# A four-layer graph network on one core: a new layout for the third layer's split values, and run masks computed in the passes before it

## The chip, the core and the metric

The kernel runs on one NeuronCore of a Trainium2 chip. The core has TensorE (PE in the profile; its weight loads are PEld), VectorE (DVE), ScalarE (ACT), GpSimd (POOL), SyncE (SP) and 16 DMA engines. They run side by side and meet only at semaphores. The metric is the device time of one execution in microseconds (us), lower is better.

## The reference

There are 6250 nodes with 64 features, and 200,000 edges sorted by their target. Four layers follow each other; each adds its result to x and normalises the rows.

```python
x = _layernorm(x + _L0_gnn_ref(x, edge_index, ...))   # mean over neighbours, two dense layers
x = _layernorm(x + _L1_gnn_ref(x, edge_index))        # neighbours weighted by 1/sqrt(deg*deg)
x = _layernorm(x + _L2_gnn_ref(x, edge_index, ...))   # the third layer
x = _layernorm(x + _L3_gnn_ref(x, edge_index, ...))   # the fourth: attention
# third layer (_L2), after Wh = h @ W + b, row, col = src, dst
dot = jnp.sum(Wr * Wc, axis=-1)
sim = dot / jnp.maximum(nr * nc, EPS)
prop_pos = jax.ops.segment_sum((base * sim_pos)[:, None] * Wc, row, num_segments=n_nodes)
prop_neg = jax.ops.segment_sum((base * sim_neg)[:, None] * Wc, row, num_segments=n_nodes)
# fourth layer (_L3)
m = jax.ops.segment_max(alpha, dst, num_segments=n)
a = jnp.exp(alpha - m[dst])
a = a / (s[dst] + 1e-16)
out = jax.ops.segment_sum(a[:, None] * x_j, dst, num_segments=n) + bias
```

## The kernel before

The nodes make 49 blocks of 128. The edges are sorted into 49 x 49 pairs of (target block, source block) with up to 128 edges each; `G` is 7, so a block is worked in 7 groups of 7 pairs, and layers three and four have 343 such steps each. Gathers and scatters are matmuls with one-hot matrices. To keep f32 accuracy, a f32 number is split into three bf16 words (its upper half, the upper half of the remainder, and the rest), each multiplied by itself and summed in PSUM.

The stages in order of time: the head with the first layer (`pairs_*`, up to about 1240 us), which also stores a count matrix `AD`, the edges' rows `ROWS` and `ROWS3`, and the one-hot matrices `OND` and `OSD` in HBM; two passes over `AD` (`passes_*`, to about 1736 us: the first sums over the neighbours for the first layer's second half, the second for the second layer), where SP loads one 1568 KB row of `AD` per step into a ring of three and PE runs 49 matmuls on it (L1047); the third layer (`pairs3_*`, to about 2680 us); the fourth (`pairs4_*`, to the end). POOL has no work in the passes.

Every engine has its own instruction list, in the order written; a wait holds all that stands behind it on that engine.

**Third layer.** At step n PE gathers the rows of both ends (`ends`, L1289 and L1296), ACT copies one end out (L1339), DVE multiplies and sums them (L1389, L1394), and DVE makes a coefficient for each edge once per block (L1402 to L1412). Group m then goes: coefficient x value, three of its seven pairs by ACT (`values`, L1348, at step m + 8) and four by POOL (`values`, L1260); POOL takes the remainder over the upper half (`rests`, L1268) and the third word (L1270), two groups in one instruction; PE multiplies with the one-hot of the sources (`spread`, L1308, at step m + 12). POOL's order is values(u), rests(u-1), values(u+1), with u a pair of groups. The three words lie as three planes of f32 in a ring of `NV3` = 6 groups in the tile `EDG`; PE reads the upper halves of each plane, so every second bf16. `values` waits until `spread` has used the group six before. One-hot matrices of the sources wait in `NOS` = 13 buffers; SP loads them (L1237). Every third one-hot matrix of the ends is made by ACT (L1329, L1331), the others by DVE (L1381).

**Fourth layer.** At step t PE gathers group t (L1668) and ACT copies it out (L1606) into a ring of 18; ACT scales seven pairs (L1627, step k + 16), DVE takes the remainder (L1817, k + 17), POOL the third word (L1655, k + 18), PE multiplies with the one-hot of the targets (L1688, k + 19). The scaled values have a ring of `NV` = 4: L1627 waits for the L1688 of four groups before. Once per block comes the chain of the softmax: the maximum over each run of equal targets is a scan (L1841) over a 49 x 128 tile, which needs two masks, one that adds -1e30 where a run begins and one that keeps the last of each run. These are made from the targets: PE turns them (L1695), ACT copies (L1613), POOL works four instructions (L1646, L1648, L1650, L1651). PE turns the scan's result and the second mask back (L1708, L1709); tiny matmuls follow (L1719, L1678) with DVE's reductions between (L1849 to L1872, L1807 to L1813), and ACT's exponential (L1617). DVE also makes one-hot matrices for two groups at a time (L1750 for the gather, L1755 for the targets).

## Time and profile before

| | us |
|---|---|
| median of 3 runs | 3594.78 (3585.97 to 3599.09) |
| the profiled execution | 3591.77 |
| its span, first to last instruction | 3590.0 |

Busy shares of the span: PE 81%, PEld 73%, DVE 81%, ACT 62%, POOL 44%. The page cuts the span in 40 slices of 90 us; the row for POOL is near zero before slice 20, the row of TensorE's clock shows 9 or 8 tenths with a few 7s. "Idle before" in a row is the time in which the engine did nothing just before that instruction, and the engine named is the one whose event ended it. The shares are means over stages with different limits, so the views by stretch are of more use than the page.

### The profile page before, as it was taken

How to read it: one execution, taken by the hardware profiler on the slowest of the kernel's cores; microseconds unless marked ns; L12 is line 12 of the kernel's file. 1: busy time of each engine (PE TensorE's matmuls, PEld its weight loads, DVE VectorE, ACT ScalarE, POOL GpSimd, SP SyncE). 2: the span in 40 equal slices, each digit the busy share in tenths (PEclk: the TensorE clock that was granted, in tenths of full speed). 3: DMA queues.
4: the chain of work that ended last, by engine and by line, in shares of the span. 5: the costliest groups of instructions: out<-in, count | busy, mean ns of one | idle time of the engine just before them, and what ended most of it. 6: DMA issues, size and time to landing. Idle time of an engine off the chain costs nothing.

```text
span 3590.0 us, 122167 instructions
## 1 busy us (share of the span) xinstructions
PE 2911.7 (81%) x50473; PEld 2637.4 (73%) x50473; DVE 2904.2 (81%) x4610; ACT 2219.8 (62%) x6003; POOL 1584.4 (44%) x1253
## 2 busy tenths in 40 slices
PE   0199999999999699899688888787768888888886
PEld 0178888888888599899677777777757777777775
DVE  7599999999999522233688888898857999999997
ACT  6334444444444400001698888898857898899887
POOL 2012222222221000000399988898964655666564
PEclk9999999999999899999899999999977888888887
DMA  8157777777777799898687877787738888888884
GB/s 221 66 157 244 237 232 234 243 237 231 234 243 236 253 370 360 330 328 320 215 279 259 264 264 248 254 271 250 257 124 302 279 278 277 276 290 274 267 278 129
DMA packets 606666, 907.43 MB, mean 253 GB/s; under 512 B 358505, under 2 KB 494858, under 8 KB 587163
## 3 DMA queue, kind: packets, MB, share of 16 engines
q1 hardware_dynamic: 583992, 800.62, 68.1%
q10 hardware_dynamic: 19763, 94.38, 7.1%
q8 instruction: 406, 6.65, 0.7%
q0 software_dynamic: 2352, 4.52, 0.3%
q14 instruction: 153, 1.25, 0.1%
HBM read 651.96 MB, written 247.40 MB: 251 GB/s over the span
## 4 chain that ended last, share of the span: by engine, by line
PE 36%; DVE 27%; ACT 14%; issue 10%; POOL 6%; DMA 5%; ACTq 1%; SPq 0%; DVEq 0%; POOLq 0%
PE ps L683 9%; PE ps L1047 8%; PE ps L709 4%; DMA U<-AD 4%; ACT U L1627 3%; POOL EDG L1268 3%; DVE EDG L1755 3%; DVE U L1817 3%; PE ps L696 3%; ACT U L569 3%; POOL EDG L1260 2%; ACT U L1329 2%; PE ps L667 2%; PE ps L1289 1%; DVE A L1389 1%
## 5 line engine op out<-in xcount | busy, mean ns | idle before, releaser
L569 ACT ACTIVATE U<-ps 128x512 bf16<-128x512 f32 (+1 forms) x637 | 356.4, 573 | 499.5 <-PE ps L696 475.5
L1627 ACT ACTIVATE U<-U,T 128x65 f32<-128x65 f32 x1806 | 460.1, 343 | 47.7 <-PE ps L1688 42.3
L1260 POOL TENSOR_TENSOR EDG<-U,edge 128x512 f32<-128x512 f32 (+1 forms) x196 | 214.3, 1098 | 584.1 <-DVE edge L1412 551.1
L1047 PE MATMUL ps<-U 128*128 128x192 bf16 x4802 | 418.5, 248 | 33.2 <-DMA U<-AD 32.8
L1047 PEld LDWEIGHTS ps<-U 128*128 128x128 bf16 x4802 | 402.8, 98 | 42.5 <-DMA U<-AD 39.2
L1655 POOL TENSOR_TENSOR U<-U 128x455 f32<-128x455 f32 x258 | 296.4, 1152 | 215.3 <-DVE U L1817 215.3
L866 DVE TENSOR_TENSOR EDG<-edge,EDG 128x1792 bf16<-128x1792 bf16 x343 | 367.5, 1083 | 14.4 <-DMA OSD<-EDG 12.0
L502 POOL DMA_INDIRECT U<-REC,nod x49 | 94.0, 1918 | 622.4 <-PE ps L638 501.2
L683 PE MATMUL ps<-U 128*128 128x98 bf16 (+1 forms) x5292 | 363.5, 223 | 4.5 <-DVE U L854 3.5
L709 PE MATMUL ps<-EDG,U 128*128 128x193 bf16 x2401 | 311.4, 249 | 51.1 <-ACT U L569 39.9
L683 PEld LDWEIGHTS ps<-U 128*128 128x128 bf16 x5292 | 341.3, 98 | 15.7 <-DVE U L854 11.9
L1296 PE MATMUL ps<-U 128*128 128x65 bf16 x7203 | 287.2, 195 | 72.3 <-DVE A L1389 71.8
L1270 POOL TENSOR_TENSOR EDG<-EDG 128x896 f32<-128x896 f32 (+1 forms) x172 | 312.4, 1817 | 13.5
L1268 POOL TENSOR_TENSOR EDG<-EDG 128x896 f32<-128x896 f32 (+1 forms) x172 | 308.6, 1794 | 11.7 <-ACT EDG L1348 11.7
L1296 PEld LDWEIGHTS ps<-U 128*128 128x128 bf16 x7203 | 252.1, 98 | 80.5 <-DVE A L1389 80.1
L1289 PE MATMUL ps<-U 128*128 128x65 bf16 x7203 | 289.6, 195 | 13.8 <-ACT U L1331 8.0
L1389 DVE TENSOR_TENSOR A<-ps,U 128x455 f32<-128x455 f32 x343 | 210.4, 622 | 95.7 <-ACT U L1339 77.0
L1289 PEld LDWEIGHTS ps<-U 128*128 128x128 bf16 x7203 | 271.3, 98 | 18.5 <-issue 10.1
L1348 ACT ACTIVATE EDG<-U,edge 128x64 f32<-128x64 f32 x1029 | 279.3, 338 | 9.0 <-PE ps L1308 6.1
L1139 DVE TENSOR_REDUCE A<-ps 128x64 f32<-128x192 f32 x98 | 34.3, 355 | 294.3 <-PE ps L1047 294.0
L854 DVE TENSOR_TENSOR U<-U 128x3920 bf16<-128x3920 bf16 (+1 forms) x132 | 263.7, 2000 | 0.0
L1381 DVE TENSOR_SCALAR U<-U,iotap 128x1792 bf16<-128x1792 bf16 x228 | 252.7, 1109 | 1.5 <-DMA U<-ROWS 1.5
(323 smaller groups left out, 7019.4 us busy)
## 6 DMA issues: line engine op xcount, KB each, us to landing
U<-ROWS SPq DMA_DIRECT2D x411, 448.0 KB, 4.7
U<-AD SPq DMA_DIRECT2D x98, 1568.0 KB, 8.6
OND<-EDG SPq DMA_DIRECT2D x343, 224.0 KB, 2.8
OSD<-EDG SPq DMA_DIRECT2D x343, 224.0 KB, 3.6
AD<-U ACTq DMA_DIRECT2D x49, 1568.0 KB, 5.6
EDG<-ROWS SPq DMA_DIRECT2D x171, 448.0 KB, 6.3
U<-OND SPq DMA_DIRECT2D x303, 224.0 KB, 5.9
U<-OSD SPq DMA_DIRECT2D x213, 224.0 KB, 4.7
```

The costliest lines, as they stand in the source:

```text
L569: ev4.by(act.activation(prow[i % NPW][:, P * g:P * (g + m)], ps[4 + gg % 2][:, 0:P * m], ACT.Copy))
L683: ins = pe.matmul(ps[3][:, o:o + NB * (f1 - f0)], w_, FR[h][:, c, f0:f1, :, k], start=(h + c + k + f0 == 0), stop=(last and f0 == 0))
L709: ins = pe.matmul(ps[6][:, 0:XW], prow[i % NPW][:, P * j:P * j + P], Xs[:, j, :], start=(j == 0), stop=(j == NB - 1))
L866: hot8.by(dve.tensor_tensor(HOT[r].rearrange("p s c (r k) -> p (s c) r k", k=2), bc(r1v.unsqueeze(1), [P, 14, D, 2]), bc(sdb[i % 2][:, b, ...
L1047: ins = pe.matmul(ps[q][:, 0:192], arow[r][:, P * j:P * j + P], (XsB if p else XsA)[:, j, :, :].rearrange("p s f -> p (s f)"), start=(j == ...
L1260: ins = pool.tensor_tensor(VD[:, v:v + w, 0, KA * D:G * D].rearrange("p w (k f) -> p w k f", f=D), W_, bc(c_.unsqueeze(3), [P, w, G - KA, ...
L1268: rem3.by(pool.tensor_tensor(VD[:, v:v + w, 1, :], VD[:, v:v + w, 0, :], VH[:, v:v + w, 0, :], ALU.subtract))
L1270: low3.by(pool.tensor_tensor(VD[:, v:v + w, 2, :], VD[:, v:v + w, 1, :], VH[:, v:v + w, 1, :], ALU.subtract))
L1289: ins = pe.matmul(ps[h][:, 65 * k:65 * k + 65], rw[r][:, 2 * P * k + P:2 * P * k + 2 * P], Ws[:, i0 + k, s_, 0:65], start=(s_ == 0), stop= ...
L1296: ins = pe.matmul(ps[2 + h][:, 65 * k:65 * k + 65], rw[r][:, 2 * P * k:2 * P * k + P], Ws[:, j, s_, 0:65], start=(s_ == 0), stop=(s_ == 2))
L1627: ins = act.activation(V4[k % NV][:, 0, c, :], H[k % NHR][:, c, :], ACT.Copy, scale=a4[d % 2][:, s:s + 1])
L1655: look.by(pool.tensor_tensor(V4[k % NV][:, 2, :, :], V4[k % NV][:, 1, :, :], S4[k % NV][:, 1, :, :], ALU.subtract))
```

## The change

Third layer. The ring holds 8 groups of 2 words per element (value and remainder side by side, 8 bytes) where it held 6 groups of 3 planes. The third word is written as bf16 into the lower half of the remainder's word, which nobody reads. So ACT and POOL write the value with a step of 8 bytes, POOL reads and writes the remainder with the same step, POOL writes 2-byte third words with a step of 8 bytes, and PE reads three adjacent bf16 of each four. The space that falls free takes two more one-hot buffers (`NOS` = 15). DVE's sum of the three words reads PSUM with the words adjacent.

Run masks. A new `passes_pool` computes both masks for all 49 blocks from `ROWS3` during the passes, seven blocks at a time, and SP stores them as bf16 in HBM (`MSK`), between its loads of `AD` in the second pass. The fourth layer loads 49 x 256 bf16 per block instead. The transposition L1695, the copy L1613 and POOL's four instructions leave it; the turning of the second mask becomes one bf16 matmul. The helpers `value_at` and `rest_at` come with empty tables, which leaves their waits as before.

```diff
+        MSK = dram("MSK", (NB, NB, 2, P), BF16)
...
+        mdst = EDG[0:NB, 0:3136].bitcast(BF16)[:, 0:NB * P].rearrange("p (d r) -> p d r", r=P)
+        mboth = EDG[0:NB, 3136:9408].bitcast(BF16).rearrange("p (d m r) -> p d m r", m=2, r=P)
+        mdif = U[0:NB, upper + NB * 96:upper + NB * 96 + GB * 129].rearrange("p (d r) -> p d r", r=129)
+        def passes_pool(pool):
+            msk_d.by(pool.memset(mdif[:, :, 0:1], 1.0))
+            msk_d.by(pool.memset(mdif[:, :, P:P + 1], 1.0))
+            pool.wait_ge(msk_ld.at, msk_ld.o + 16)
+            for g in range(NGB):
...
+                msk_d.by(pool.tensor_tensor(mdif[:, :, 1:P], mdst[:, bl, 1:P], mdst[:, bl, 0:P - 1], ALU.subtract))
+                pool.wait_ge(msk_d.at, msk_d.o + 4 * g + 3)
+                msk_d.by(pool.tensor_scalar(mdif, mdif, 0.0, 1.0, ALU.is_equal, ALU.subtract))
+                pool.wait_ge(msk_d.at, msk_d.o + 4 * g + 4)
+                msk_ok.by(pool.tensor_scalar(mboth[:, bl, 0, :], mdif[:, :, 0:P], BIG, None, ALU.mult))
+                msk_ok.by(pool.tensor_scalar(mboth[:, bl, 1, :], mdif[:, :, 1:P + 1], -1.0, None, ALU.mult))
+            pool.wait_ge(msk_st.at, msk_st.o + 16 * NGB)
         def passes_sp(sp):
+            msk_ld.by(sp.dma_start(mdst, ROWS3[1].rearrange("d (s r) -> s d r", r=P)), 16)
             for p in range(2):
                 for i in range(NB):
+                    if p and i % GB == GB - 1:
+                        g = i // GB
+                        sp.wait_ge(msk_ok.at, msk_ok.o + 2 * g + 2)
+                        msk_st.by(sp.dma_start(MSK[GB * g:GB * g + GB].rearrange("d s m r -> s d (m r)"),
+                                               mboth[:, GB * g:GB * g + GB, :, :].rearrange("p d m r -> p d (m r)")), 16)
...
-        NV3 = 6
-        VD = EDG[:, 0:3 * G * D * NV3].rearrange("p (v s e) -> p v s e", v=NV3, s=3)
-        VH = EDG[:, 0:3 * G * D * NV3].bitcast(BF16).rearrange("p (v s e h) -> p v s e h", v=NV3, s=3, h=2)[:, :, :, :, 1]
+        NV3 = 8
+        VD = EDG[:, 0:2 * G * D * NV3].rearrange("p (v e w) -> p v e w", v=NV3, w=2)
+        VH = EDG[:, 0:2 * G * D * NV3].bitcast(BF16).rearrange("p (v e h) -> p v e h", v=NV3, h=4)
...
-                rem3.by(pool.tensor_tensor(VD[:, v:v + w, 1, :], VD[:, v:v + w, 0, :], VH[:, v:v + w, 0, :], ALU.subtract))
+                rem3.by(pool.tensor_tensor(VD[:, v:v + w, :, 1], VD[:, v:v + w, :, 0], VH[:, v:v + w, :, 1], ALU.subtract))
                 pool.wait_ge(rem3.at, rem3.o + u + 1)
-                low3.by(pool.tensor_tensor(VD[:, v:v + w, 2, :], VD[:, v:v + w, 1, :], VH[:, v:v + w, 1, :], ALU.subtract))
+                low3.by(pool.tensor_tensor(VH[:, v:v + w, :, 2], VD[:, v:v + w, :, 1], VH[:, v:v + w, :, 3], ALU.subtract))
...
-                    ins = pe.matmul(ps[4 + j % 2][:, 0:3 * D], OSn[m % NOS][:, k, :], S3[m % NV3][:, :, k, :], start=(i == 0), stop=(i == NB - 1))
+                    ins = pe.matmul(ps[4 + j % 2][:, 0:3 * D], OSn[m % NOS][:, k, :], VH[:, m % NV3, D * k:D * k + D, 1:4], start=(i == 0), stop=(i == NB - 1))
...
-                    ins = act.activation(V3[m % NV3][:, 0, k, :], Wc[:, j % 2, i0 + k, 0:D], ACT.Copy, scale=edge[:, 6 + j % 2, i0 + k:i0 + k + 1])
+                    ins = act.activation(VD[:, m % NV3, D * k:D * k + D, 0], Wc[:, j % 2, i0 + k, 0:D], ACT.Copy, scale=edge[:, 6 + j % 2, i0 + k:i0 + k + 1])
...
+            def run_masks(d):
+                if d >= 2:
+                    sp.wait_ge(ytr.at, ytr.o + d - 1)
+                mk_ld[d % 2].by(sp.dma_start(masks[d % 2], MSK[d]), 16)
...
-                    ytr.by(pe.transpose(ps[3][:, 64:64 + NB], lastf, ident[0:NB, 0:NB]))
+                    ytr.by(pe.matmul(ps[3][:, 64:64 + NB], masks[d % 2][:, 1, :], identh, start=True, stop=True))
...
-                    dvf.by(dve.tensor_tensor_scan(ysc, negs, ps[2][0:NB, 0:P], -BIG, ALU.add, ALU.max))
+                    dve.wait_ge(mk_ld[d % 2].at, mk_ld[d % 2].o + 16 * (d // 2 + 1))
+                    dvf.by(dve.tensor_tensor_scan(ysc, masks[d % 2][:, 0, :], ps[2][0:NB, 0:P], -BIG, ALU.add, ALU.max))
```

## Rows read from the trace of the kernel before

**Rows 1.** Busy time by stretch: passes, third layer, a steady 100 us, fourth layer.

```profile
core 0: us, PE busy (x) PEld busy (x) DVE busy (x) ACT busy (x) POOL busy (x), PEclk, DMA share, GB/s
1240.00:1480.00 240.00, 212.92 (x2469) 206.62 (x2470) 75.02 (x162) 16.70 (x35) 0.00 (x0) 0.96 0.91 350
1480.00:1736.00 256.00, 230.27 (x2483) 216.74 (x2480) 88.36 (x225) 26.19 (x79) 0.00 (x0) 0.96 0.82 300
1753.00:2665.00 912.00, 722.79 (x16548) 688.60 (x16549) 762.18 (x1111) 795.74 (x1678) 824.22 (x540) 0.97 0.77 254
1790.00:1890.00 100.00, 80.80 (x1972) 78.57 (x1973) 85.78 (x124) 92.21 (x191) 95.98 (x64) 1.00 0.83 279
...
2740.00:3540.00 800.00, 660.30 (x13553) 607.26 (x13554) 753.28 (x1706) 717.12 (x2661) 482.94 (x502) 0.88 0.84 277
```

**Rows 2.** Groups by line, 1753 to 2665 us, POOL, then one of ACT.

```profile
L1270 POOL TENSOR_TENSOR EDG<-EDG 128x896 f32<-128x896 f32 (+1 forms) x172 | 312.4, 1817 | 13.5
L1268 POOL TENSOR_TENSOR EDG<-EDG 128x896 f32<-128x896 f32 (+1 forms) x172 | 308.6, 1794 | 11.7 <-ACT EDG L1348 11.7
L1260 POOL TENSOR_TENSOR EDG<-U,edge 128x512 f32<-128x512 f32 (+1 forms) x196 | 214.3, 1098 | 584.1 <-DVE edge L1412 551.1 <-PE ps L1308 32.7
...
L1348 ACT ACTIVATE EDG<-U,edge 128x64 f32<-128x64 f32 x1029 | 279.3, 338 | 9.0 <-PE ps L1308 6.1 <-DVE edge L1412 2.9
```

**Rows 3.** Waits in the same stretch, POOL: total, times, longest, in us.

```profile
POOL EDG L1260 <- PE ps L1308: 32.7, 23, 5.3
```

**Rows 4.** Groups by line and shape in the first 150 us: ACT, then DVE.

```profile
L255 ACT ACTIVATE U<-U 128x1568 bf16<-128x1568 int32 x1 | 7.2, 7175 | 0.0
...
L251 ACT ACTIVATE EDG<-EDG 128x1568 f32<-128x1568 f32 x1 | 1.5, 1510 | 0.0
...
L401 DVE TENSOR_TENSOR U<-EDG,U 128x1568 f32<-128x1568 f32 x1 | 3.0, 2980 | 8.2 <-ACT U L261 8.2
...
L386 DVE TENSOR_TENSOR EDG<-EDG,A 128x1568 f32<-128x1568 f32 x1 | 1.8, 1791 | 0.0
```

**Rows 5.** Groups by line, 2740 to 3540 us (46 blocks): POOL, then DVE.

```profile
L1655 POOL TENSOR_TENSOR U<-U 128x455 f32<-128x455 f32 x238 | 275.7, 1161 | 191.7 <-DVE U L1817 191.7
...
L1648 POOL TENSOR_SCALAR MISC<-T 49x129 f32<-49x129 f32 x46 | 39.5, 860 | 4.0
L1646 POOL TENSOR_TENSOR T<-MISC 49x127 f32<-49x127 f32 x46 | 33.7, 732 | 10.0 <-ACT MISC L1613 9.6
L1651 POOL TENSOR_SCALAR T<-MISC 49x128 f32<-49x128 f32 x46 | 30.5, 663 | 3.6
L1650 POOL TENSOR_SCALAR T<-MISC 49x128 f32<-49x128 f32 x46 | 24.4, 530 | 3.8
...
L1755 DVE TENSOR_SCALAR EDG<-EDG,iotap 128x1792 bf16<-128x1792 bf16 x160 | 149.8, 936 | 5.4 <-DMA EDG<-ROWS 5.4
```

**Rows 6.** Timeline of one block's mask work and what follows, DVE, then POOL.

```profile
3152.91 2.77 DVE L1755 TENSOR_SCALAR EDG<-EDG,iotap 128x1792 bf16<-128x1792 bf16 x1
...
3152.44 0.94 POOL L1651 TENSOR_SCALAR T<-MISC 49x128 f32<-49x128 f32 x1
3153.35 0.94 POOL L1655 TENSOR_TENSOR MISC<-MISC 128x455 f32<-128x455 f32 x1
3154.25 0.94 POOL L1655 TENSOR_TENSOR U<-U 128x455 f32<-128x455 f32 x1
```

**Rows 7.** Timeline: the passes' first loads and matmuls, and two small stores of ROWS.

```profile
1241.20 3.12 SPq L999 DMA_DIRECT2D U<-AD  x3
...
1248.75 1.46 PE L1047 MATMUL ps<-U 128*128 128x192 bf16 x8 [14.78 <-DMA U<-AD]
...
1226.59 0.27 ACTq L558 DMA_DIRECT2D ROWS<-EDG  x1
1226.89 1.25 ACTq L559 DMA_DIRECT2D ROWS<-EDG  x1
```

**Rows 8.** The line L1755: count, duration in ns as minimum/median/maximum.

```profile
L1755 DVE TENSOR_SCALAR EDG<-EDG,iotap x172: 442/681/2770, 2702.9 to 3553.2; 128x1792 bf16<-128x1792 bf16 x171, 128x896 bf16<-128x896 bf16 x1
```

More of the change, by code:

```diff
@@ L1496, in cell @@
             return rows[k // 2 % n][:, e:e + P]
-        seg, negs, lastf, ylast = (Tflat[0:NB, 1225 + 130 * n:1225 + 130 * n + w] for n, w in enumerate((129, P, P, P)))
+        ylast = Tflat[0:NB, 1615:1615 + P]
+        masks = [MISC[0:NB, 1365 + P * i:1365 + P * i + P].bitcast(BF16).rearrange("p (m r) -> p m r", m=2) for i in range(2)]
+        identh = ident[0:NB, 0:NB].bitcast(BF16).rearrange("p (r h) -> p r h", h=2)[:, :, 1]
         ysc = ps[3][0:NB, P:2 * P]
@@ L1533, in due4, with value_at, rest_at @@
             return (k // G, k % G, k) if 0 <= k < NT else (None, None, None)
+        GV, GR = (), ()
+        def value_at(eng, k):
+            d, g = k // G, k % G
+            if g in GV:
+                eng.wait_ge(vop.at, vop.o + d * len(GV) + GV.index(g) + 1)
+            else:
+                eng.wait_ge(vok.at, vok.o + d * (G - len(GV)) + sum(h not in GV for h in range(g + 1)))
+        def rest_at(eng, k):
+            d, g = k // G, k % G
+            if g in GR:
+                eng.wait_ge(rop.at, rop.o + d * len(GR) + GR.index(g) + 1)
+            else:
+                eng.wait_ge(rok.at, rok.o + d * (G - len(GR)) + sum(h not in GR for h in range(g + 1)))
         def block4(t, off):
@@ L1578, in pairs4_sp @@
                     hots(k)
+                d = block4(t, 2)
+                if d is not None and d >= 2:
+                    run_masks(d)
                 d = block4(t, 40)
@@ L1607, in pairs4_act @@
                                           ps[k % 2][:, 0:65 * G].rearrange("p (k f) -> p k f", f=65), ACT.Copy))
-                d = block4(t, 6)
-                if d is not None:
-                    act.wait_ge(dtr.at, dtr.o + d + 1)
-                    if d:
-                        act.wait_ge(flg.at, flg.o + 2 * d)
-                    dcp.by(act.activation(dcol, ps[2][0:NB, P:2 * P], ACT.Copy))
                 d = block4(t, 16)
@@ L1618, in pairs4_act @@
                 d, g, k = due4(t, 16)
-                if k is not None:
+                if k is not None and g not in GV:
                     act.wait_ge(exo.at, exo.o + d + 1)
@@ L1814, in pairs4_dve @@
                 d, g, k = due4(t, 17)
-                if k is not None:
-                    dve.wait_ge(vok.at, vok.o + k + 1)
+                if k is not None and g not in GR:
+                    value_at(dve, k)
                     rok.by(dve.tensor_tensor(V4[k % NV][:, 1, :, :], V4[k % NV][:, 0, :, :], S4[k % NV][:, 0, :, :], ALU.subtract))
```

56 lines of the change are left out of this document (20 added, 36 removed).

## The prediction

> **What bounds the kernel now.** I read the busy time by stretch first [rows 1]. The passes are held by TensorE and the loads of `AD`: PE is busy 213 of 240 us in the first pass and 230 of 256 in the second, with DMA at 0.91 and 0.82, and POOL has nothing to do. In the third layer POOL has the most work, 824 of 912 us; in a steady 100 us it is busy 96, with ACT at 92, DVE at 86 and PE at 81. In the fourth layer DVE leads, 753 of 800 us (94%), before ACT with 717 (90%), PE 660, POOL 483. So a saving counts in the third layer only if POOL gets work done earlier, and in the fourth only if DVE does. The reader is to see that POOL is the least busy of the four where its mask work is taken out, and the busiest where its layout changes.
>
> **Third layer, the ring of eight.** POOL's three lines take 312 + 309 + 214 = 835 us, 4.86 us for each of 172 pairs of groups [rows 2]. Its idle time inside the layer is 912 - 824 = 88 us [rows 1]: 11.7 for ACT's values, 32.7 for PE's spread of the group six before, in 23 waits of 1.4 us each [rows 2, 3], and most of the rest for the coefficient (in the row of L1260 that wait holds the passes too, which is why it shows 551). Only the last is the ring. With eight places `values(u)` may start two groups earlier, but `rests(u)` behind it still waits for ACT's values, which ACT makes at step m + 8, as before. So one L1260 per stall, 1.10 us, can be done beforehand: at most 23 x 1.10 = 25 us, at least nothing, where the stall was DVE's delay and POOL then waits for ACT or the coefficient. I take 10, nearer the lower end, since a ring only smooths. ACT's wait on the same ring is 6.1 us [rows 2], and the two more one-hot buffers relieve SP, which has idle time in every step; both cost or give nothing by themselves. In all -10 (0 to -25).
>
> **Third layer, the steps of 8 bytes.** ACT's L1348 (1029 x 0.27 us busy), POOL's L1260, L1268 and L1270 and PE's moving operand of L1308 keep their counts and sizes, only their addresses change. No row has a step of 8 bytes. From below: nothing, since L1268 and L1270 already read a bf16 of every 4 bytes and take 1.79 / 896 = 2.0 ns an element, while L1260, which reads packed f32, takes 1.10 us for at most 512, so 2.1 ns or more [rows 2]. A gain is excluded, as no element is saved. From above: a step of 20 bytes. DVE reading one operand so (L401) took 2.98 us for 1568 elements against 1.79 packed (L386), 0.76 ns more an element; ACT writing bf16 so (L255) took 7.2 us against 1.5 for packed f32 (L251), 3.6 ns more an element [rows 4]. I take nothing: 8 bytes are nearer to 4, which costs nothing, than to 20, and POOL's 2 ns an element leave a memory port more time than DVE's 1.1. If it does cost, it costs on POOL, which has no cover: this is the main rival.
>
> Two pages of the Trainium skill speak to it and disagree. "GPSIMD Engine Reference", section "Performance pitfalls for Q7 kernels", says that GpSimd's reads slow from about 1.9 to 2.9 cycles an element once the step exceeds 8 bytes, and this change stops exactly at 8; by that page the term is nothing. "Vector Engine (DVE) Microarchitecture Reference", section "Measured stream behaviour on trn2", says that a port keeps its rate only with runs of two adjacent 4-byte words; by that page every stream here would pay about 0.65 cycle an element. The row of L401 agrees with the second for 20 bytes; neither page gives 2-byte writes by GpSimd.
>
> **Passes, the added work.** In front of the first load of `AD` SP issues one DMA of 2401 pieces of 256 bytes (615 KB). PE's start hangs on that queue: the first three loads were issued from 1241.2 on and PE started at 1248.75, released by the DMA [rows 7]. So its time lands on the path. Its transfer at the 350 GB/s of that stretch [rows 1] is 1.8 us; its issue lies between 0.3 us (L558, 49 rows in one piece) and, if the 0.98 us by which L559 with its 98 pieces is longer grows with the pieces, 24 us [rows 7]. I take +4, nearer to the lower end, as the issue of L559 is one row only and its pieces are strided in HBM. In the second pass SP stores 7 x 176 KB; at 300 GB/s 4.1 us of DMA time beside a stretch where DMA is at 0.82 and PE at 90% [rows 1]; behind each store waits the load of `AD` for three rows later, so it is hidden. POOL's masks there: four instructions of some 900 elements and two memsets seven times, at 2 ns an element [rows 2] about 7 x 7 = 50 us of an engine that idles 500. Nobody but SP's stores waits for it, and the first wait comes after a whole pass. Bounds 0 to +26, taken +4.
>
> **Fourth layer, the masks.** POOL's four instructions are 39.5 + 33.7 + 30.5 + 24.4 = 128 us in 46 blocks, 2.8 us a block [rows 5]. POOL is not the bound, so this is not the gain. What counts is what stands behind them: two L1655 become ready while POOL works on masks and then run without a pause, and a DVE instruction that wants the memory at that time waits for both. The timeline shows it: L1755 began at 3152.91, when L1651 was running, and ended at 3155.68, 2.77 us, behind L1655 at 3153.35 and 3154.25 [rows 6]. Its median is 0.68 us [rows 8]. Ten of the 46 blocks have such a row at 2.77, which makes 10 x 2.09 = 21 us, and three more an L1817 held in the same way. Summing for every block how much L1750, L1755, L1817, L1830 and L1854 exceed their quickest, by the time since L1646 began, gives 2.9 us a block, of which 1.0 us falls in the third microsecond, where the backlog runs, and 0.1 in the first; mean L1755 is 0.936 us for the same reason [rows 5]. Upper bound: 1.1 us go for good, 49 x 1.1 = 54 us. Lower bound: the two L1655 now collide as the other five do, (2.9 - 1.1) / 5 = 0.36 us each, so 1.1 - 0.7 = 0.4 us, 49 x 0.4 = 20 us; and nothing, if the collisions only move. I take 0.6 us a block, 29 us. It lands on the end because DVE is 94% busy. What is late next: ACT, 90% busy, whose L1627 waits for the spread that stands behind the same backlog; it also loses its copy. PE loses one f32 transposition per block and nothing waits on it. The new loads are 25 KB a block in SP's queue, asked for at step 7d + 2 and used by DVE at 7d + 9, seven steps of 2.5 us later; SP's wait for the turned mask of block d - 2 is past by then. Behind that wait stand the one-hot loads of SP, three steps ahead, so a short wait would be covered too. The two loads at the layer's start are two issues of 0.3 us (as L558 [rows 7]) before the first edge rows, inside the rounding of the sum.
>
> **The sum.** +4 in the passes, -10 in the third layer, -29 in the fourth: -35 us. The profiled execution took 3591.8, which gives 3557; it stands 3 us under the median of 3594.8, which gives 3560. I predict 3560, with 3535 to 3585 as the case's own range (ends of the terms partly added: -29 -25 -9 and +10 -15 -5).
>
> **The rivals.**
> *The backlog goes for good.* The upper ends of both gains: +4 - 20 - 54 = -70, 3525. For it: ACT's waits behind the spread lie in the same microseconds and go too. Against it: seven L1655 per block remain and each needs DVE's absence. 12%.
> *The collisions only move.* DVE's excess stays 2.9 us a block, and the ring's slack is taken by ACT's fixed step m + 8: +4 - 4 - 5, about 3590. For it: POOL's seven L1655 are 75% of its work in that layer (483 - 128 = 355 us of 483 [rows 1, 5]). Against it: the 2.77 us rows need two L1655 in a row. 18%.
> *POOL slows on the step of 8 bytes, the case on the other side.* Place: L1268 and L1270, 172 pairs of 896 elements. Price by the row of L401: 0.76 ns x 896 x 2 = 1.36 us a pair; POOL's idle time in the layer (88 us, 0.5 a pair [rows 1]) takes some, so 146 to 234 us more, less the 25 of the other two terms: 3716 to 3804, of which I take the lower end, and by the row of L255 on the third word alone far more. It decides from 35 / 172 = 0.2 us a pair, 0.11 ns an element. For it: POOL is 96% busy in steady stretches, nothing hides a longer instruction; the 2-byte writes have only L255 beside them. The page on the DVE cited above would give the same sign. Against it: steps of 4 bytes cost nothing now. 20%, spread from a few tens of us up; a mild form ends near 3620.
>
> **How the numbers follow.** The forecast's case has 50%, the three rivals 12, 18 and 20. A measurement of this kernel can tell about 0.5%, 18 us, from no change: under 3577 counts as faster, over 3613 as slower. Faster: 12 + about 46 of the first case's 50 = 58%. Same: 4 + 18 - 1 = 21%. Slower: 20% and 1 for a long issue of the first mask load = 21%. The range of 8 in 10 starts at 3522, which leaves some 6% below, and ends at 3640, which leaves about 13% of the slow case's 20 above.
>
> **What would show it.** Right: L1268 and L1270 near 1.8 us as before; no L1755 of 2.77 us in the fourth layer and its mean under 0.9; blocks of about 16.9 us where they were 17.5 (800 / 46, from [rows 5]); PE's first matmul of the passes some 4 us after where it was; POOL idle before L1260 for the spread nearly gone. Wrong: L1268 or L1270 over 2 us, or L1348 over 0.34; L1755 unchanged in its mean while POOL's busy time fell by 128 us; a wait of DVE for the mask load; a gap of over 10 us at the passes' start.

## The result, and the profile after

The changed kernel took 3637.17 us (median of 4 runs, 3630.59 to 3643.48) against 3593.37 us for the kernel before (4 runs), a ratio of 1.012 with a 95% interval of 1.011 to 1.014. It is 44 us slower where 35 us less were forecast. Its profiled span is 3634.8 us, 44.8 more than the span before, so the two traces hold the whole difference.

The line numbers move. In the third layer: L1260, L1268, L1270 of POOL are now L1289, L1297, L1299; PE's spread L1308 is L1337, ACT's value L1348 is L1377. In the passes L1047 is L1078; in the fourth layer L1750, L1755, L1817, L1655 are L1779, L1784, L1846, L1692.

First the busy time by stretch, the view of [rows 1]: passes, third layer, a steady 100 us of it, fourth layer.

```profile
core 0: us, PE busy (x) PEld busy (x) DVE busy (x) ACT busy (x) POOL busy (x), PEclk, DMA share, GB/s
1240.00:1480.00 240.00, 210.77 (x2462) 206.08 (x2463) 80.86 (x162) 16.70 (x35) 71.81 (x42) 0.95 0.91 352
...
1756.00:2738.00 982.00, 785.46 (x16554) 723.90 (x16555) 821.35 (x1110) 801.21 (x1678) 910.69 (x540) 0.95 0.73 236
1790.00:1890.00 100.00, 80.49 (x1794) 75.57 (x1792) 84.89 (x117) 86.31 (x173) 96.51 (x58) 0.98 0.79 259
2812.00:3592.00 780.00, 653.18 (x13623) 605.97 (x13619) 705.56 (x1719) 716.39 (x2645) 370.18 (x323) 0.88 0.87 288
```

The same 540 POOL instructions of the third layer now fill 911 us of 982, where they filled 824 of 912. In the steady 100 us POOL is as busy as before (96.5), but gets through 58 instructions instead of 64, and DVE and ACT through fewer as well. In the fourth layer DVE does 1719 instructions in 706 us, where it did 1706 in 753, and ACT, 716 us of 780, is now busier than DVE.

The groups of POOL by line in the third layer, then one of ACT, as in [rows 2]:

```profile
L1299 POOL TENSOR_TENSOR EDG<-EDG 128x896 bf16<-128x896 f32 (+1 forms) x172 | 407.2, 2367 | 13.5
L1297 POOL TENSOR_TENSOR EDG<-EDG 128x896 f32<-128x896 f32 (+1 forms) x172 | 309.8, 1801 | 14.1 <-ACT EDG L1377 14.1
L1289 POOL TENSOR_TENSOR EDG<-U,edge 128x512 f32<-128x512 f32 (+1 forms) x196 | 229.9, 1178 | 474.9 <-DVE edge L1441 473.9 <-PE ps L1337 1.0
...
L1377 ACT ACTIVATE EDG<-U,edge 128x64 f32<-128x64 f32 x1029 | 281.0, 344 | 6.2 <-PE ps L1337 4.4 <-DVE edge L1441 1.7
```

One of the two long instructions is as it was (1.80 us); the one that writes bf16 went from 1.82 to 2.37 us. The stage boundaries give the account. The next two fences are one line each of the two kernels, before and after: count, then the minimum, median and maximum duration in ns, then the first and last start. The first line of each is DVE's comparison that opens the third layer, the second its last sum.

```profile
L1381 DVE TENSOR_SCALAR U<-U,iotap x228: 671/931/2156, 1734.0 to 2629.9; 128x1792 bf16<-128x1792 bf16 x114
L1449 DVE TENSOR_REDUCE ps<-ps x49: 346/353/367, 1784.7 to 2666.5; 128x64 f32<-128x192 f32 x49
```

```profile
L1410 DVE TENSOR_SCALAR U<-U,iotap x228: 670/1197/2778, 1737.2 to 2698.6; 128x1792 bf16<-128x1792 bf16 x114
L1478 DVE TENSOR_REDUCE ps<-ps x49: 345/352/367, 1788.9 to 2738.4; 128x64 f32<-128x192 f32 x49
```

Up to the third layer +3.2 us (1734.0 to 1737.2). The third layer, from the one line's first start to the other's last, 932.5 to 1001.2: +68.7. From there to the end of the span 923.5 to 896.4: -27.1. The sum is +44.8. Two of the three stages did what was forecast; the third layer did not. I use this measure of a stage for every kernel below.

### The profile page after: what moved, and what is told of

Same layout as the page of the kernel before. It is cut to its first block, busy times and chain, and to the rows that moved or that the text cites. A ratio compares the mean times of both kernels' runs of the same rounds, so it can differ in the third digit from the quotient of the medians.

```text
span 3634.8 us, 121775 instructions
## 1 busy us (share of the span) xinstructions
PE 2958.6 (81%) x50424; PEld 2665.6 (73%) x50424; DVE 2913.0 (80%) x4608; ACT 2217.0 (61%) x5954; POOL 1616.6 (44%) x1099
## 4 chain that ended last, share of the span: by engine, by line
PE 37%; DVE 22%; ACT 14%; issue 11%; POOL 9%; DMA 7%; ACTq 1%; SPq 0%; DVEq 0%; POOLq 0%
PE ps L684 9%; PE ps L1078 7%; PE ps L710 4%; DMA U<-AD 4%; POOL EDG L1297 4%; ACT U L1679 3%; POOL EDG L1289 3%; ACT U L570 3%; PE ps L697 3%; DVE U L1846 2%; DMA EDG<-ROWS 2%; PE ps L668 2%; POOL EDG L1299 1%; PE ps L1715 1%; DVE EDG L1784 1%
## 5 line engine op out<-in xcount | busy, mean ns | idle before, releaser
L1692 POOL TENSOR_TENSOR U<-U 128x455 f32<-128x455 f32 x258 | 304.2, 1181 | 350.1 <-DVE U L1846 350.1
L1078 PE MATMUL ps<-U 128*128 128x192 bf16 x4802 | 417.4, 248 | 36.6 <-DMA U<-AD 36.3
L1289 POOL TENSOR_TENSOR EDG<-U,edge 128x512 f32<-128x512 f32 (+1 forms) x196 | 229.9, 1178 | 474.9 <-DVE edge L1441 473.9
L1078 PEld LDWEIGHTS ps<-U 128*128 128x128 bf16 x4802 | 402.8, 98 | 44.7 <-DMA U<-AD 41.7
L1299 POOL TENSOR_TENSOR EDG<-EDG 128x896 bf16<-128x896 f32 (+1 forms) x172 | 407.2, 2367 | 13.5
L684 PEld LDWEIGHTS ps<-U 128*128 128x128 bf16 x5292 | 341.5, 98 | 15.9 <-DVE U L855 12.3
L1325 PE MATMUL ps<-U 128*128 128x65 bf16 x7203 | 292.0, 196 | 57.3 <-DVE A L1418 57.2
L1297 POOL TENSOR_TENSOR EDG<-EDG 128x896 f32<-128x896 f32 (+1 forms) x172 | 309.8, 1801 | 14.1 <-ACT EDG L1377 14.1
L1318 PE MATMUL ps<-U 128*128 128x65 bf16 x7203 | 295.9, 197 | 11.9 <-ACT U L1360 8.0
L1325 PEld LDWEIGHTS ps<-U 128*128 128x128 bf16 x7203 | 257.5, 99 | 62.9 <-DVE A L1418 62.9
L1410 DVE TENSOR_SCALAR U<-U,iotap 128x1792 bf16<-128x1792 bf16 x228 | 298.8, 1311 | 0.0
L1318 PEld LDWEIGHTS ps<-U 128*128 128x128 bf16 x7203 | 280.8, 100 | 22.3 <-issue 8.2
L1377 ACT ACTIVATE EDG<-U,edge 128x64 f32<-128x64 f32 x1029 | 281.0, 344 | 6.2 <-PE ps L1337 4.4
L1368 ACT ACTIVATE U<-ps 128x455 f32<-128x455 f32 x343 | 185.4, 541 | 146.0 <-PE ps L1318 144.7
```

The costliest lines, as they stand in the source:

```text
L684: ins = pe.matmul(ps[3][:, o:o + NB * (f1 - f0)], w_, FR[h][:, c, f0:f1, :, k], start=(h + c + k + f0 == 0), stop=(last and f0 == 0))
L1078: ins = pe.matmul(ps[q][:, 0:192], arow[r][:, P * j:P * j + P], (XsB if p else XsA)[:, j, :, :].rearrange("p s f -> p (s f)"), start=(j == ...
L1289: ins = pool.tensor_tensor(VD[:, v:v + w, KA * D:G * D, 0].rearrange("p w (k f) -> p w k f", f=D), W_, bc(c_.unsqueeze(3), [P, w, G - KA, ...
L1297: rem3.by(pool.tensor_tensor(VD[:, v:v + w, :, 1], VD[:, v:v + w, :, 0], VH[:, v:v + w, :, 1], ALU.subtract))
L1299: low3.by(pool.tensor_tensor(VH[:, v:v + w, :, 2], VD[:, v:v + w, :, 1], VH[:, v:v + w, :, 3], ALU.subtract))
L1318: ins = pe.matmul(ps[h][:, 65 * k:65 * k + 65], rw[r][:, 2 * P * k + P:2 * P * k + 2 * P], Ws[:, i0 + k, s_, 0:65], start=(s_ == 0), stop= ...
```

## The experiments

All times are medians beside runs of the kernel before on the same chip (its median lies between 3588.5 and 3591.1 there, and at 3593.4 beside the changed kernel); a ratio is to the runs beside it, and small differences between kernels are read from the ratios too. The stages are from the profiled execution, and one execution scatters by some 5 us, so a stage counts only where the medians agree.

**The two halves of the change, each alone.** masks_only is the kernel before with the masks from the passes, layout_only the kernel before with the third layer of the changed one.

> Only the run masks from the passes; the third layer as before. If the two halves of the change are independent (theory A), the passes lose some 3 us, the third layer is unchanged (930 us from PE's first gather to DVE's last sum) and the fourth gains 27 us, as in the changed kernel: 3593 + 3 - 27 = about 3569 us. If the fourth layer's gain came with the longer third layer, which starts the fourth at another point of the DMA queues (theory B), it stays near 3590 us.

> Only the third layer's layout, ring of eight and fifteen one-hot buffers; the masks as before. Theory A: the third layer takes 69 us more, the rest is unchanged: about 3662 us, with the third word's instruction on POOL at 2.37 us mean against 1.82 and the remainder's at 1.80. Theory B, in which masks and layout disturb each other (POOL's work in the passes, the waits at the start of the third layer): less than 50 us more, below 3643 us.

masks_only took 3576.2 us (ratio 0.9958, 0.9943 to 0.9973), layout_only 3654.6 (1.018, 1.016 to 1.020). The stages of masks_only: third layer 934.3, rest 899.5. Of layout_only: 1000.1 and 921.7. So the halves don't touch each other, and all of the loss is the layout's. By the medians the masks are worth 12 us alone (15 by the ratio). On top of the layout they are worth 22 us, each kernel against the kernel before beside it: layout_only is 66.0 us over its own (3654.6 - 3588.5), the changed kernel 43.8 over its own. The profiled executions show 21 and 17 by their whole spans. The stages of all kernels scatter less. After the third layer, the four with mask work on POOL or a stand-in for it (the kernel before, layout_only, and bf16_planar and pool_busy below) take 920.0 to 923.5 us, and the seven without it and with nothing added there 896.3 to 902.8. The masks are worth some 22 us of that stage.

**Which property of the layout.** bf16_planar is the kernel before, with the third word written as bf16 into its own plane, at 4 bytes from one to the next:

```diff
-low3.by(pool.tensor_tensor(VD[:, v:v + w, 2, :], ...
+low3.by(pool.tensor_tensor(VH[:, v:v + w, 2, :], ...
```

word4 is the changed kernel, with the third word written as f32 over the remainder, 8 bytes from one to the next (the second word is then lost and left out of the sum):

```diff
-low3.by(pool.tensor_tensor(VH[:, v:v + w, :, 2], ...
+low3.by(pool.tensor_tensor(VD[:, v:v + w, :, 1], ...
```

> The kernel before, with one edit: POOL writes the third word as bf16 into the upper half of its own plane, a step of 4 bytes, where it wrote f32. Theory W (a 2-byte write by POOL is slow by itself): the instruction goes to 2.2 us undisturbed from 1.68, 2.37 mean from 1.82, and the kernel to some 3593 + 172 x 0.55 = up to 3688 us, less what idle time POOL has (88 us in the layer, some 40 of it usable): 3650 to 3688. Theory S (2-byte writes are slow only with the step of 8 bytes): the instruction stays at 1.68 and 1.82 us and the kernel at 3593 us.

> The changed kernel, with one edit: POOL's third-word instruction writes its result as f32 over the remainder (same reads, same step of 8 bytes, 4-byte words). The second word is left out of the sum, so the output is less exact; all counts are the same. Theory W or S (the 2-byte write costs): the instruction falls back to 1.68 us undisturbed and 1.82 mean, and the third layer loses the 69 us: 3637 - 69 = 3568 us, or some 10 less if the ring of eight is worth something. Rival R (the reads with steps of 8 bytes or PE's slower reading of three of four bf16 cost): the instruction stays at 2.4 or the kernel above 3610 us.

bf16_planar took 3589.9 us (ratio 1.000, 0.999 to 1.001), word4 3582.6 (0.998, 0.997 to 1.000). The line of the third word in the kernel before, in bf16_planar, in the changed kernel and in word4 (durations as above):

```profile
L1270 POOL TENSOR_TENSOR EDG<-EDG x172: 932/1682/2179, 1763.4 to 2663.7; 128x896 f32<-128x896 f32 x171, 128x448 f32<-128x448 f32 x1
```

```profile
L1270 POOL TENSOR_TENSOR EDG<-EDG x172: 937/1942/2185, 1759.1 to 2662.1; 128x896 bf16<-128x896 f32 x171, 128x448 bf16<-128x448 f32 x1
```

```profile
L1299 POOL TENSOR_TENSOR EDG<-EDG x172: 1301/2444/2809, 1765.5 to 2735.5; 128x896 bf16<-128x896 f32 x171, 128x448 bf16<-128x448 f32 x1
```

```profile
L1299 POOL TENSOR_TENSOR EDG<-EDG x172: 933/1939/2177, 1765.9 to 2677.1; 128x896 f32<-128x896 f32 x171, 128x448 f32<-128x448 f32 x1
```

The minimum is the one instruction of 448 elements: 0.93 us in three kernels, 1.30 in the changed one. The medians of the other three hop between 1.68 and 1.94, two levels that depend on where DVE stands: of the 84 long ones in the kernel before that took 1.9 us or more, 76 started while DVE's L1381 was running, of the 87 that took 1.7 none. In the changed kernel the same two levels lie at 2.2 and 2.45. The means are 1.82, 1.83 and 1.82 us, against 2.37. So neither the 2-byte write nor the step of 8 bytes costs by itself; both together do. From word4 to the changed kernel the third layer grows from 942.4 to 1001.2 us: 59 of the 69 us are this one instruction. The 172 instructions take 172 x 0.54 = 93 us more; POOL's busy time in the layer grows by 86 (825.2 to 910.7 us), since a little of the instruction lies beside the next one, and POOL's idle time, 117 us in word4, gives back 27. word4 took 3582.6 us where I had expected 3568: its third layer is still 10 us longer than in the kernel before, of which 5 can be PE's read, as said below, and the rest I can't place.

**The price by itself.** steps adds 90 subtractions of 896 elements to the passes, where POOL is idle.

```diff
+        def passes_pool(pool):
+            st_.by(pool.memset(EDG[:, 0:8064], 1.0))
...
+                st_.by(pool.tensor_tensor(<output, one step>, EDG[:, 0:896], EDG[:, 896:1792], ALU.subtract))
```

> The kernel before, with 90 GpSimd instructions added in the two passes, where GpSimd has nothing to do: fifteen forms of the same tensor_tensor subtraction of 896 elements, each six times, one after the other, on otherwise unused columns of EDG. All inputs and the output are packed f32, except that one of them has a step: output f32 at 4, 8, 12, 16 bytes; output bf16 at 2, 4, 6, 8, 12, 16 bytes; first input f32 at 8 and 12 bytes; second input bf16 at 4, 8, 12 bytes. Nothing is left out; the time of the kernel is not what is asked. Theory S (the step and the size of a write together are what costs): bf16 written at 8 bytes takes 2.2 us, every f32 write 1.7 us, bf16 at 4 bytes 1.7 us. Theory W (any 2-byte write costs) is then wrong. Two forms of S differ: if each partly written 8-byte word costs, bf16 at 8, 12 and 16 bytes take the same 2.2 us and 6 bytes something between; if the distance counts, it grows from 8 to 12 to 16 bytes. Rival from the reading side (steps beyond 8 bytes): f32 and bf16 read at 12 bytes take half as long again, 2.5 us, and those read at 8 bytes 1.7.

POOL's timeline of the first of six rounds (start, duration). L1001 to L1007 write f32 at 8, 12 and 16 bytes; L1010 to L1025 write bf16 at 2, 4, 6, 8, 12 and 16 bytes. L1028 reads the first input at 8 bytes.

```profile
1250.83 2.35 POOL L1001 TENSOR_TENSOR EDG<-EDG 128x896 f32<-128x896 f32 x1
1253.26 2.11 POOL L1004 TENSOR_TENSOR EDG<-EDG 128x896 f32<-128x896 f32 x1
1255.45 2.10 POOL L1007 TENSOR_TENSOR EDG<-EDG 128x896 f32<-128x896 f32 x1
1257.63 2.08 POOL L1010 TENSOR_TENSOR EDG<-EDG 128x896 bf16<-128x896 f32 x1
1259.79 2.08 POOL L1013 TENSOR_TENSOR EDG<-EDG 128x896 bf16<-128x896 f32 x1
1261.95 2.09 POOL L1016 TENSOR_TENSOR EDG<-EDG 128x896 bf16<-128x896 f32 x1
1264.12 2.21 POOL L1019 TENSOR_TENSOR EDG<-EDG 128x896 bf16<-128x896 f32 x1
1266.41 3.21 POOL L1022 TENSOR_TENSOR EDG<-EDG 128x896 bf16<-128x896 f32 x1
1269.71 4.20 POOL L1025 TENSOR_TENSOR EDG<-EDG 128x896 bf16<-128x896 f32 x1
1273.99 2.13 POOL L1028 TENSOR_TENSOR EDG<-EDG 128x896 f32<-128x896 f32 x1
```

The first round is the one to read, because DVE is nearly idle there from L1004 on. In the later rounds DVE runs instructions with two inputs beside it, and L1010 takes 2.33 us. Its six executions (durations as above), then DVE and POOL in the second round:

```profile
L1010 POOL TENSOR_TENSOR EDG<-EDG x6: 2081/2330/2339, 1257.6 to 1450.4; 128x896 bf16<-128x896 f32 x6
```

```profile
1293.57 2.40 DVE L1207 TENSOR_TENSOR T<-X,dis 128x448 f32<-128x448 f32 x1
1295.58 2.33 POOL L1010 TENSOR_TENSOR EDG<-EDG 128x896 bf16<-128x896 f32 x1
```

L1010 starts while DVE's L1207 is still running and is 0.25 us longer. The 2.35 of L1001 above is the same thing: in all six rounds a DVE instruction with two inputs was running when it started. The packed f32 form (L998, 2.54 to 2.85 us) has no undisturbed row either.

Undisturbed, a bf16 write takes 1.00 us more for each 4 bytes of distance from 8 bytes on (2.21, 3.21, 4.20), that is 0.28 ns a byte and some 0.2 us; an f32 write takes 2.1 us at 12 and 16 bytes, and at 8 bytes no more than 2.35. My 1.7 us for the f32 writes and for bf16 at 4 bytes was wrong. Up to 6 bytes the bf16 write is hidden under what the instruction takes anyway, 2.08 us here, so steps alone has only 0.13 us for the 8 bytes, and beside DVE nothing (2.21 where 2, 4 and 6 bytes take 2.33 to 2.35). In the third layer the same instruction takes 1.68 us, and the same 2.21 us of writing show as 0.53 us more. Why it is shorter there is not shown. A bf16 input is not the reason, since L1034, which has one at 4 bytes, also takes 2.08 us; in the layer both inputs lie in the same words, which steps doesn't try. The second of my two forms was right: the distance counts, not the partly written word. And the price doesn't come from writing into a word that is just being read: steps writes to other columns and takes the same 2.21 us.

The reading rival is weak. The first input as f32 took 2.13 us at 8 bytes and 2.36 at 12 (undisturbed), the second as bf16 2.08, 2.38 and 2.58 at 4, 8 and 12 (medians); the last two started beside DVE in all six rounds, so some 0.25 us of each is DVE's by estimate. That leaves some 12% more at 12 bytes, and not half as long again.

**Steps of 12 bytes, and PE's order.** three is the changed kernel with three f32 side by side, ring of six, thirteen one-hot buffers.

```diff
-        VD = EDG[:, 0:2 * G * D * NV3].rearrange("p (v e w) -> p v e w", v=NV3, w=2)
+        VD = EDG[:, 0:3 * G * D * NV3].rearrange("p (v e w) -> p v e w", v=NV3, w=3)
...
-low3.by(pool.tensor_tensor(VH[:, v:v + w, :, 2], ...
+low3.by(pool.tensor_tensor(VD[:, v:v + w, :, 2], ...
...
-  VH[:, m % NV3, D * k:D * k + D, 1:4]
+  VH[:, m % NV3, D * k:D * k + D, 1:6:2]
```

> The changed kernel with value, remainder and third word as f32 side by side, 12 bytes to an element, with the ring of six and thirteen one-hot buffers as before the change; PE then reads every other bf16 of a run of six, a constant step of 4 bytes, in the same order (element, then word) as in the changed kernel. The result is complete. Theory: only the 2-byte write at 8 bytes and the read of three of four bf16 cost. Then both of GpSimd's instructions take 1.8 us and the seven matmuls of the spread 0.76 us at full clock, as in the kernel before, the third layer 933 us and the kernel 3576, as with the masks alone. Rival R12, steps beyond 8 bytes slow GpSimd's reads by half (what the Trainium skill states in GPSIMD Engine Reference, section Performance pitfalls for Q7 kernels; the estimate from it is 2.7 us for each of the two): 172 x 1.8 = 310 us less the 88 us of idle time that GpSimd has, so about 3790. Rival F: the order (element, then word) by itself slows PE, and the matmuls take 0.93 us: third layer 942, kernel 3586.

It took 3592.5 us (ratio 1.000, 0.999 to 1.001), 16 more than masks_only, so neither my 3576 nor the rival's 3790. (Its profiled execution took 3602.0, so the stage below is on the long side.) POOL's two long instructions, as groups by line:

```profile
L1299 POOL TENSOR_TENSOR EDG<-EDG 128x896 f32<-128x896 f32 (+1 forms) x172 | 326.0, 1895 | 13.5
L1297 POOL TENSOR_TENSOR EDG<-EDG 128x896 f32<-128x896 f32 (+1 forms) x172 | 324.3, 1885 | 11.3 <-ACT EDG L1377 11.3
```

Against 1.82 and 1.79 us that is 0.17 us a pair, 172 x 0.17 = 29 us, and the third layer is 24.5 us longer than in masks_only (958.8 to 934.3). The Trainium skill ("GPSIMD Engine Reference", section "Performance pitfalls for Q7 kernels") puts a cost on reads with a step beyond 8 bytes, half as long again. The place agrees with the trace: 8 bytes cost nothing in word4, 12 bytes do here and in steps (2.13 to 2.36 us). The size doesn't, for this instruction with two inputs: 5% here, where the write is at 12 bytes too, and 11% in steps.

PE settles the other question. Its spread of one group (7 matmuls of 192 columns), near the start of the layer at full clock, in the timelines of the kernel before, the changed kernel and three:

```profile
1793.22 0.76 PE L1308 MATMUL ps<-EDG,MISC 128*128 128x192 bf16 x7
```

```profile
1793.28 0.92 PE L1337 MATMUL ps<-EDG 128*128 128x192 bf16 x7
```

```profile
1794.04 0.76 PE L1337 MATMUL ps<-EDG 128*128 128x192 bf16 x7
```

The order (element, then word) is free at a constant step of 4 bytes; reading three of every four bf16 costs 0.16 us a group, 343 x 0.16 = 55 us of PE's time. It is hardly on the path: word6 below has it, its third layer is 5 us longer than that of masks_only (939.6 to 934.3), and its median is no higher (3574.1 to 3576.2).

**The ring.** word6 is word4 with six places, ring6 the changed kernel with six places (`NV3 = 6`, nothing else).

> As word4 (the third word written as f32 over the remainder, the second word left out), with the ring of six places instead of eight. word4 took 3582.6 and its third layer 942 us from the first gather to the last sum, where the kernel before has 932. Theory P: the ring of eight gave nothing, since the wait that it removes (32.7 to 1.2 us) came back as a wait for ACT's values (11.7 to 37.2 us), and the 10 us too many come from PE's slower read of three of every four bf16: then word6 takes the same within 3 us, 3580 to 3586, and the wait for PE's spread is back at about 30 us while that for ACT falls to about 12. Rival, by the forecast: the ring is worth 10 us and PE's read costs 20, so word6 takes 3592 or more, and its third layer 952.

> The changed kernel with the ring of six places instead of eight, nothing else. The changed kernel took 3637.2, its third layer 1001 us from the first gather to the last sum; with the third word as f32 the ring of eight moved the third layer from 940 (word6) to 942 (word4), so nothing. Theory N (the ring gives nothing, since GpSimd is the bound and ACT's values, made at a fixed step, come next): 3630 to 3642, a wait for PE's spread of some 20 to 40 us, and as much less for ACT's values or the coefficient. Rival, by the forecast: with the slower third word the ring still saves its 10 us, so without it 3645 to 3650.

word6 took 3574.1 us (ratio 0.9952, 0.9935 to 0.9969), 8.5 less than word4 and below the 3580 that I had expected; ring6 3638.3 (1.0132, 1.0115 to 1.015), the same as the changed kernel within the intervals. The third layer is 939.6 us in word6 and 942.4 in word4, 1006.1 in ring6 and 1001.2 in the changed kernel. So the ring of eight lost 3 us in one pair and gained 5 in the other, no more than one execution scatters. POOL's waits in the third layer tell why (total, times, longest). First word6, then word4, whose first row also holds the one wait of 435.9 us through the passes:

```profile
POOL EDG L1289 <- PE ps L1337: 39.5, 27, 5.5
POOL EDG L1289 <- DVE edge L1441: 29.3, 19, 3.2
...
POOL EDG L1297 <- ACT EDG L1377: 12.0, 13, 5.7
```

```profile
POOL EDG L1289 <- DVE edge L1441: 480.5, 22, 435.9
...
POOL EDG L1297 <- ACT EDG L1377: 37.2, 26, 5.6
...
POOL EDG L1289 <- PE ps L1337: 1.2, 1, 1.2
```

With six places 39.5 + 29.3 + 12.0 = 80.8 us; with eight 1.2 + 44.6 + 37.2 = 83.0 us. The wait for the spread went, and the same time is now waited for ACT's values, made at their fixed step, and for the coefficient. In ring6 and the changed kernel the same three sum to 64.6 and 56.7 us. The pair also prices the third word once more: from word6 to ring6 the third layer grows by 66.5 us, where it was 59 with the ring of eight. The 8.5 us between the medians of word4 and word6 lie only for 3 us in the third layer; the rest I can't place.

**Where the masks' gain comes from.** pool_busy is masks_only with four instructions a block of the old sizes put back on POOL in the fourth layer, on unused columns, with nobody waiting for them.

```diff
+                d = block4(t, 7)
+                if d is not None:
...
+                    xd.by(pool.tensor_tensor(xt_[:, 1:P], xs_[:, 1:P], xs_[:, 0:P - 1], ALU.subtract))
+                    xd.by(pool.tensor_scalar(xs_[:, 0:129], xt_, 0.0, 1.0, ALU.is_equal, ALU.subtract))
+                    xd.by(pool.tensor_scalar(Tflat[0:NB, 1485:1613], xs_[:, 0:P], BIG, None, ALU.mult))
+                    xf.by(pool.tensor_scalar(xt_[:, 0:P], xs_[:, 1:P + 1], -1.0, None, ALU.mult))
```

> The masks from the passes and the third layer as before (masks_only: 3576.2), with four GpSimd instructions a block put back into the fourth layer at the step where the mask work stood, of the same sizes and kinds, on unused columns; nobody waits for them. Theory B (as forecast: GpSimd's mask work and the backlog behind it held up DVE): most of the gain goes, DVE's mean for its one-hot comparison rises from about 0.71 us to about 0.94, with single ones at 2.77 us, and the kernel takes 3590 to 3605. Rival C: the gain came from the shorter chain (ACT's copy, PE's transposition and the scan's input gone), not from GpSimd's absence: 3574 to 3580, and the mean stays near 0.71.

It took 3595.9 us (ratio 1.001, 1.000 to 1.002): 20 us over masks_only, all of the gain. The stage after the third layer is 920.0 us, nearly as before the change (923.5), and DVE is busy 733 of the 780 us from 2760 to 3540, as in the kernel before (734) and not as in masks_only (705). So the shorter chain (ACT's copy, PE's transposition) is worth nothing that shows, at most the 3.5 us between the two stages, and POOL's absence the rest. The line L1755 of the kernel before in the changed kernel, then in pool_busy:

```profile
L1784 DVE TENSOR_SCALAR EDG<-EDG,iotap x172: 441/680/1367, 2774.9 to 3598.0; 128x1792 bf16<-128x1792 bf16 x171, 128x896 bf16<-128x896 bf16 x1
```

```profile
L1804 DVE TENSOR_SCALAR EDG<-EDG,iotap x172: 443/680/1422, 2709.4 to 3556.1; 128x1792 bf16<-128x1792 bf16 x171, 128x896 bf16<-128x896 bf16 x1
```

No row of 2.77 us in either, yet pool_busy lost its 20 us. What carries the cost is not the pile of two L1655 that I picked out, but many small collisions: from 2790 to 3540 us, the means of L1787, L1782 (on U) and L1849 (on U) of masks_only are 723, 883 and 705 ns, those of the same lines of pool_busy 774, 1008 and 773.

**Two attempts to do better.** late_load is masks_only with the first mask load behind three rows of `AD`; rem_pool gives one of seven remainders a block to POOL in the fourth layer (`GR = (3,)`); both does both.

```diff
-            msk_ld.by(sp.dma_start(mdst, ROWS3[1].rearrange("d (s r) -> s d r", r=P)), 16)
             for p in range(2):
...
+                    if p == 0 and i == NA:
+                        msk_ld.by(sp.dma_start(mdst, ROWS3[1].rearrange("d (s r) -> s d r", r=P)), 16)
```

```diff
+                d, g, k = due4(t, 17)
+                if k is not None and g in GR:
+                    value_at(pool, k)
+                    rop.by(pool.tensor_tensor(V4[k % NV][:, 1, :, :], V4[k % NV][:, 0, :, :], S4[k % NV][:, 0, :, :], ALU.subtract))
```

> The masks from the passes, third layer as before (masks_only: 3576.2), with the load of the two-byte target rows of the masks issued behind the first three rows of AD instead of in front of them. Theory: that load (0.36 us of issue and its transfer in front of the row that PE waits for) is what costs the passes 3 to 5 us; the first matmul of the passes then starts where it did before, at about 1246 to 1249 us, and the kernel takes 3571 to 3574. Rival: the passes are held by the total of their loads, so that the 615 KB cost the same wherever they stand, and nothing changes: 3575 to 3578.

> The masks from the passes, third layer as before (masks_only: 3576.2), and in the fourth layer one of the seven remainders of a block is made by GpSimd instead of DVE. DVE is the busiest engine there (705 of 780 us), GpSimd has 367. DVE loses 49 x 0.70 = 34 us, GpSimd gains 49 x 1.2 = 57 us. Theory: DVE sets the pace and GpSimd's work costs DVE by its collisions, which pool_busy put at 20 us for about 128 us of added work, so 9 us here: -34 + 9 = -25, 3551. Rival A (ACT, 713 of 780 us, is the next bound): at most 1% is left above ACT, 3565 to 3570. Rival B (two GpSimd instructions of 455 elements then run one behind the other, and DVE waits for both, as behind the masks): no gain or a loss, 3576 to 3590.

> late_load and rem_pool together: masks from the passes with their load behind the first three rows of AD, third layer as before, and one of seven remainders of the fourth layer on GpSimd. late_load took 3571.7 and rem_pool 3566.7, against 3576.2 for masks_only. Theory: the two lie in different stages and add, so 3576 - 4.5 - 9.5 = 3562, between 3557 and 3567. Rival: the 4.5 us of late_load is scatter of the passes (the first gather of the third layer came at 1734.2 there, at 1735.4 in masks_only, while the first matmul came 3.7 us earlier), and nothing adds: 3565 to 3570.

late_load took 3571.7 us (ratio 0.9948, 0.9934 to 0.9962), rem_pool 3566.7 (0.9943, 0.9927 to 0.9958), both 3567.6 (0.9937, 0.9922 to 0.9951). Each is faster than the kernel before by 0.5 to 0.6%; their intervals overlap, and against masks_only (0.9958) only a few us are gained. In late_load PE's first matmul of the passes is back at 1245.92, from 1249.61 in masks_only, but the third layer opens 1.2 us earlier only (1734.2 to 1735.4), and in the kernel both the move adds nothing: the passes gave most of it back. rem_pool gained 5 us by the ratio and 9 by the medians, not 25. Its fourth layer, 2760 to 3540 us, below that of masks_only in the same stretch:

```profile
2760.00:3540.00 780.00, 647.02 (x13479) 596.85 (x13477) 704.73 (x1712) 712.59 (x2634) 367.16 (x323) 0.89 0.85 282
```

```profile
2760.00:3540.00 780.00, 651.48 (x13473) 598.37 (x13472) 699.42 (x1669) 722.75 (x2674) 413.66 (x376) 0.88 0.84 281
```

ACT, which was already a little busier than DVE in masks_only (713 to 705 us), takes 723 of 780 us, and DVE's 43 fewer instructions take only 5 us less, since the others got longer beside POOL (L1853, its remainder on U, 738 ns for 707): rival A, with some of B.

## Why the prediction was wrong

*What bounds the kernel.* Right for POOL in the third layer: its time there grew by 911 - 824 = 86 us, its idle time fell by 88 - 71 = 17 [rows 1], and the difference is the +69 of the layer. In the fourth DVE is the one that POOL's work delays (pool_busy), but once the masks are gone ACT is as busy as DVE, as I had named it next; rem_pool ran into it.

*Ring of eight, -10.* Too large: +3 in one pair and -5 in the other, nothing that the runs can tell from zero. The wait went as said (32.7 us [rows 3] to 1.0), and came back in word4 in full, in the changed kernel in part (the coefficient 29 to 42 us, ACT's values 12 to 14), the lower bound that I had named. With word4 and word6 the sum of POOL's waits is 83 and 81 us. A slot more in a ring helps only if what fills the slot can also run ahead, and ACT's step was fixed.

*Steps of 8 bytes, 0.* This step failed, and it alone turns the sign. I put four edits (a read, an f32 write, a 2-byte write, PE's read) under one term and argued it from the step. The read and the f32 write leave POOL's durations as they were (1.78 and 1.82 us in word4). The 2-byte write costs 0.55 us a pair in the mean, 59 us on the layer (word4 to the changed kernel). A row that hinted at it was there: L255, ACT writing bf16 at 20 bytes, 7.2 us against 1.5 [rows 4]; I used it as a far upper bound, because 8 is nearer to 4 than to 20. By the line through the rows of steps, the price shows from some 6 bytes on ((1.68 - 0.2) / 0.25 us a byte, an estimate), so that 8 is already past the point. My second reason, that 2 ns an element leave a port time to spare, is the right picture with the wrong number: at 8 bytes the write takes 2.21 us for 896 elements, 2.5 ns each. The rival had the right place and sign, and a price (1.36 us a pair from L401, a read) 2.5 times too large; its "mild form near 3620" was the nearest thing to the result of 3637. My own sign for it, L1270 over 2 us, is what the trace shows (2.37). It deserved more than 20%, as the one term with a known bad row, on the engine without cover.

*PE's read.* I had said that its cost was nothing; it is 0.16 us a group. It stays beside POOL's work, at most 5 us.

*Passes, +4.* Right: +3.2 us. The start of the third layer scatters (1729.8 to 1734.0 us in the three kernels without the masks, 1734.6 to 1741.0 in the eight with the load in front), and by the two means it is 5.6. SP's issue of the load took 0.36 us, near the lower of my bounds (0.3 and 24), and PE's first matmul came 4.9 us later (1248.75 [rows 7] to 1253.65), in masks_only only 0.9 (1249.61). POOL's masks took 71.8 us where I said 50, hidden as said.

*Fourth layer, -29.* Nearly right in size: -27.1 in this pair of traces, some -22 over all kernels, and 12 to 22 us by the medians for masks and passes together, where my two terms give 25. The 2.77 us are gone, L1755's mean fell from 936 to 715 ns, a block from 17.4 us (I had written 17.5) to 17.0. But the reason was half right: in pool_busy the cost is back without the 2.77 us, so it is POOL's time beside DVE as such.

## What to carry to other kernels

Before a layout is changed, list each stream apart with its direction, the bytes of one element and the distance between two, and price each from its own row; a 2-byte write on POOL has its own price from 8 bytes on in these runs, and it grows with the distance. If the only row for a stream is a bad one far off, that is a warning and not an outer bound. And a wait for a buffer is worth its time only if the producer behind it can start earlier as well: read who would be waited for next before the gain is booked.
